# Grouped-query attention: value products in three parts, normalising on GpSimd, the first merge between turned pieces

## The reference, cut to what matters

```python
q = (hidden_states @ Wq).reshape(B, S, nh, hd).transpose(0, 2, 1, 3)
k = (hidden_states @ Wk).reshape(B, S, nkv, hd).transpose(0, 2, 1, 3)
v = (hidden_states @ Wv).reshape(B, S, nkv, hd).transpose(0, 2, 1, 3)
...
q = _apply_rope(q, cos, sin)
k = _apply_rope(k, cos, sin)
...
logits = jnp.einsum('bhqd,bhkd->bhqk', q, k) * scale
...
logits = jnp.where(causal[None, None], logits, neg)
attn = jax.nn.softmax(logits.astype(jnp.float32), axis=-1).astype(q.dtype)
out = jnp.einsum('bhqk,bhkd->bhqd', attn, v)
...
return out @ Wo
```

## Time and profile before

| | before |
|---|---|
| median of 3 runs | 2662.03 us (2660.21 to 2664.17) |
| the profiled execution | 2660.67 us |
| its span in the trace | 2658.9 us |
| busy: TensorE, VectorE, ScalarE, GpSimd | 96%, 59%, 42%, 17% |
| grouped-query stage in the trace | from about 1768 to 2593 us |

### The profile page before, as it was taken

How to read it: one execution, slowest core, us unless ns; L and a number is a source line. 1 busy time by engine, 2 the same in 40 slices (tenths; PEclk the granted TensorE clock), 3 DMA queues, 4 the chain that set the end, 5 groups by cost and what they waited for, 6 DMA issues and landing times. The chain is left out here.

```text
span 2658.9 us, 38579 instructions
## 1 busy us (share of the span) xinstructions
PE 2546.1 (96%) x12487; PEld 1843.6 (69%) x12487; DVE 1573.6 (59%) x2919; ACT 1128.3 (42%) x1832; POOL 440.4 (17%) x519
## 2 busy tenths in 40 slices
PE   6999999999999999999998779989999999999996
PEld 3666666666666666666665456667878878778774
DVE  5666666666666666666664631057557557566566
ACT  3455555555555555555554310024324324334231
POOL 0101010101010010101010000014334334343310
PEclk8899999999999999999999789989999999999998
DMA  5122121222222221212221320010010010010001
GB/s 192 42 48 53 42 50 42 53 43 50 47 45 50 44 56 42 50 42 51 45 51 51 108 73 0 0 72 24 24 39 16 24 39 16 24 39 5 12 0 52
DMA packets 46693, 116.86 MB, mean 44 GB/s; under 512 B 5313, under 2 KB 22721, under 8 KB 40514
## 3 DMA queue, kind: packets, MB, share of 16 engines
q1 hardware_dynamic: 46658, 116.40, 16.6%
HBM read 71.81 MB, written 10.49 MB: 31 GB/s over the span
## 5 line engine op out<-in xcount | busy, mean ns | idle before, releaser
L407 DVE TENSOR_REDUCE row_max<-ps_max 128x1 f32<-128x512 f32 x1024 | 672.3, 688 | 234.1 <-PE ps_max L472 204.4
L361 ACT ACTIVATE probs<-ps_score 128x1024 f32<-128x1024 f32 x512 | 525.6, 1027 | 123.6 <-PE ps_score L487 94.2
L485 PE MATMUL ps_score<-Q,K 128*128 128x512 f32 x1024 | 409.0, 399 | 0.5 <-ACT probs L361 0.5
L487 PE MATMUL ps_score<-Q,K 97*128 97x512 f32 x1024 | 405.6, 396 | 0.0
L472 PE MATMUL ps_max<-KX,Q 68*128 68x512 f32 x1024 | 379.9, 412 | 4.5 <-DVE row_max L407 2.5
L401 DVE TENSOR_TENSOR Q<-ps_x,Q 64x512 fp32r<-64x512 f32 x256 | 176.5, 690 | 240.3 <-ACT Q L356 238.5
L356 ACT ACTIVATE Q<-ps_x 64x512 fp32r<-64x512 f32 x256 | 152.0, 594 | 379.6 <-PE ps_x L457 378.2
L472 PEld LDWEIGHTS ps_max<-KX,Q 68*128 68x128 f32 x1024 | 189.1, 189 | 110.2 <-issue 53.0
L497 PE MATMUL ps_o<-probs,V_slot 128*32 128x512 f32 x2048 | 233.0, 595 | 1.1 <-ACT probs L361 1.1
L485 PEld LDWEIGHTS ps_score<-Q,K 128*128 128x128 f32 x1024 | 194.2, 190 | 55.2 <-ACT probs L361 13.3
L487 PEld LDWEIGHTS ps_score<-Q,K 97*128 97x128 f32 x1024 | 194.8, 190 | 40.9
(11 more groups left out here) (217 smaller groups left out, 3906.6 us busy)
## 6 DMA issues: line engine op xcount, KB each, us to landing
Q<-Q SPq DMA_DIRECT2D x64, 512.0 KB, 4.3
w_raw<-in_w_qrope SPq DMA_DIRECT2D x32, 512.0 KB, 3.7
wq_raw<-in_wq SPq DMA_DIRECT2D x8, 1024.0 KB, 5.6
wo_raw<-in_wo SPq DMA_DIRECT2D x8, 1024.0 KB, 4.9
w_raw<-in_w SPq DMA_DIRECT2D x6, 704.0 KB, 4.1
Q<-content_q SPq DMA_DIRECT2D x64, 64.0 KB
K<-content_k SPq DMA_DIRECT2D x64, 64.0 KB
wkv_raw<-in_wkv SPq DMA_DIRECT2D x8, 512.0 KB, 3.6
```

What stands on the lines that cost most here:

```text
L361: act.activation(probs[:, j, 2 * half:2 * half + 2, :], ps_score[half][:, :, :], ACT.Exp, scale=SCALE).then_inc(exped, 1)
L407: dve.tensor_reduce(row_max[:, t, j:j + 1], ps_max[t % 2][:, :], axis=AXX, op=ALU.max)\
L485: pe.matmul(ps_score[half][:, k, :], K1[:, b, t * P:(t + 1) * P], Q1[:, b, j, :], start=True, stop=False)
L487: last = pe.matmul(ps_score[half][:, k, :], K2[0:MROW + 1, b, j, t * P:(t + 1) * P], Q2[0:MROW + 1, b, j, :], start=False, stop=True)
```

## The change

Four things are changed, all in `gqa_stage`.

1. The values and the turned probabilities are kept in high and low parts. ScalarE's copies now write the high parts; VectorE subtracts them from PSUM to make the low ones (`low_values`, two per head, and `low_turned`, three per unit). `outputs` makes twelve fp32r matmuls per unit in place of four fp32 ones. The third turned piece and the matmuls with low probabilities wait for the low parts (`t_low`).
2. The multiplication of the probabilities with the reciprocals moves from VectorE (`normalise`) to GpSimd, with four instructions of the same widths. VectorE keeps the reciprocals (`invert`).
3. In GpSimd's list `normalise` of unit u − 2 stands behind `rope_query` of unit u; that of units 6 and 7 stands behind the loop over units.
4. The third turned piece of unit 7 stands between merge 0 and merge 1, on VectorE between the two additions to `X`.

```diff
-        V = buf("v1", [P, NB, ST, P])
+        V = [buf(f"v_{k}", [P, NB, ST, P], F32R) for k in ("hi", "lo")]
...
-        probsT = buf("probsT", [P, 3, S])
+        TURNED = [(0, S), (S, S), (2 * S, 2 * P)]
+        probsT = [buf(f"probsT_{k}", [P, 2 * S + 2 * P], F32R) for k in ("hi", "lo")]
...
+            def normalise(i, u):
+
+                pool.wait_ge(inverted, i + 1)
+                pool.sem_inc(gate_pool, 1)
+                for t in range(ST):
+                    n = (t + 1) * P
+                    ins = pool.tensor_scalar(probs[:, u % 2, t, 0:n], probs[:, u % 2, t, 0:n], inverse[:, u % 2, t:t + 1],
+                                             None, ALU.mult)
+                ins.then_inc(normed, 1)
...
                 for u in range(2, NU):
                     pool.wait_ge(scored, NU * kv + u - 1)
                     rope_query(r + u - 2, u, u % 2)
+                    normalise(NU * kv + u - 2, u - 2)
...
-                if not last:
-                    for b in range(NB):
+                for b in range(NB):
+                    normalise(NU * kv + NU - 2 + b, NU - 2 + b)
+                    if not last:
                         pool.wait_ge(scored, NU * kv + NU - 1 + b)
                         rope_key(r + NU - 2 + 2 * b, b)
                         rope_query(r + NU - 1 + 2 * b, b, 1)
...
-            def normalise(i, u):
+            def invert(i, u):
                 dve.wait_ge(exped, ONE + ST * (i + 1))
-                dve.reciprocal(inverse[:, :], sums[:, u % 2, :]).then_inc(inverted, 1)
-                dve.wait_ge(inverted, i + 1)
-                for t in range(ST):
-                    n = (t + 1) * P
-                    ins = dve.tensor_scalar(probs[:, u % 2, t, 0:n], probs[:, u % 2, t, 0:n], inverse[:, t:t + 1],
-                                            None, ALU.mult)
-                ins.then_inc(normed, 1)
+                dve.reciprocal(inverse[:, u % 2, :], sums[:, u % 2, :]).then_inc(inverted, 1)
...
+            def low_turned(i, u, k):
+                dve.wait_ge(t_high, 3 * i + k + 1)
+                at, n = TURNED[k]
+                dve.tensor_tensor(probsT[1][:, at:at + n], ps_t[(u + k) % 2][:, 0:n], probsT[0][:, at:at + n],
+                                  ALU.subtract).then_inc(t_low, 1)
...
                 maxima(i)
-                normalise(i, 0)
+                invert(i, 0)
+                for b in range(NB):
+                    low_values(kv, b)
                 rope(r, ring + ring_query(2), (START + ring_query(2)) % 2, 0, tk, 0)
                 for u in range(1, NU):
                     maxima(i + u)
-                    normalise(i + u, u)
+                    low_turned(i + u - 1, u - 1, 0)
+                    low_turned(i + u - 1, u - 1, 1)
+                    invert(i + u, u)
+                    low_turned(i + u - 1, u - 1, 2)
...
+                for k in range(2):
+                    low_turned(i + NU - 1, NU - 1, k)
                 add_out(0)
+                low_turned(i + NU - 1, NU - 1, 2)
                 add_out(1)
...
-                    pe.wait_ge(t_taken, 3 * i + 1)
+                    pe.wait_ge(t_low, 3 * i + 1)
...
-                for k, piece in enumerate(pieces):
-                    pe.wait_ge(t_taken, 3 * i + k + 1)
-                    for tile, at in piece:
-                        last = pe.matmul(ps_o[:, tile * P:S], V[:, b, tile, :], probsT[:, k, at:at + S - tile * P],
-                                         start=tile == 0, stop=k == 2)
+                for p, vs in ((0, (0, 1)), (1, (0,))):
+                    for k, piece in enumerate(pieces):
+                        pe.wait_ge((t_high, t_low)[p], 3 * i + k + 1)
+                        for v in vs:
+                            for tile, at in piece:
+                                at += TURNED[k][0]
+                                last = pe.matmul(ps_o[:, tile * P:S], V[v][:, b, tile, :],
+                                                 probsT[p][:, at:at + S - tile * P],
+                                                 start=tile == p == v == 0, stop=k == 2 and p == 1)
...
-                for k in range(3):
+                for k in range(2):
                     turn(i + NU - 1, NU - 1, k)
                 pe.wait_ge(wo_split, GQ * (kv + 1))
                 pe.wait_ge(o_low, ONE + i + NU - 1)
                 merge(last, tk, 0)
+                turn(i + NU - 1, NU - 1, 2)
                 merge(last, tk, 1)
```

More of the change, by code:

```diff
@@ L1019, in gqa_stage @@
         sums = buf("sums", [P, 2, ST])
-        inverse = buf("inverse", [P, ST])
+        inverse = buf("inverse", [P, 2, ST])
         mask = buf("mask_sb", [P, 2, P], F32R)
@@ L1043, in gqa_stage @@
         v_turned = sem("v_turned")
-        v_ready = sem("v_ready")
+        v_high = sem("v_high")
+        v_low = sem("v_low")
         summed = sem("summed")
@@ L1053, in gqa_stage @@
         turned = sem("turned")
-        t_taken = sem("t_taken")
+        t_high = sem("t_high")
+        t_low = sem("t_low")
         pv_made = sem("pv_made")
@@ L1193, in values @@
                 act.wait_ge(made, START + PER * kv + b + 1)
-                act.activation(probsT[:, b, :], ps_r[(START + b) % 2][:, :], ACT.Copy).then_inc(v_taken, 1)
+                act.activation(values_T[:, b, :], ps_r[(START + b) % 2][:, :], ACT.Copy).then_inc(v_taken, 1)
             def turned_values(kv, b):
                 act.wait_ge(v_turned, NB * kv + b + 1)
-                act.activation(V[:, b, :, :], ps_t[b][:, :].rearrange("p (t n) -> p t n", t=ST), ACT.Copy)\
-                   .then_inc(v_ready, 1)
+                act.activation(V[0][:, b, :, :], ps_t[b][:, :].rearrange("p (t n) -> p t n", t=ST), ACT.Copy)\
+                   .then_inc(v_high, 1)
             def softmax(i, u):
@@ L1269, in maxima, with low_values @@
                                       negate=True).then_inc(maxed, 1)
-            def normalise(i, u):
+            def invert(i, u):
                 dve.wait_ge(exped, ONE + ST * (i + 1))
-                dve.reciprocal(inverse[:, :], sums[:, u % 2, :]).then_inc(inverted, 1)
-                dve.wait_ge(inverted, i + 1)
-                for t in range(ST):
-                    n = (t + 1) * P
-                    ins = dve.tensor_scalar(probs[:, u % 2, t, 0:n], probs[:, u % 2, t, 0:n], inverse[:, t:t + 1],
-                                            None, ALU.mult)
-                ins.then_inc(normed, 1)
+                dve.reciprocal(inverse[:, u % 2, :], sums[:, u % 2, :]).then_inc(inverted, 1)
+            def low_values(kv, b):
+                dve.wait_ge(v_high, NB * kv + b + 1)
+                dve.tensor_tensor(V[1][:, b, :, :], ps_t[b][:, :].rearrange("p (t n) -> p t n", t=ST), V[0][:, b, :, :],
+                                  ALU.subtract).then_inc(v_low, 1)
+            def low_turned(i, u, k):
+                dve.wait_ge(t_high, 3 * i + k + 1)
+                at, n = TURNED[k]
+                dve.tensor_tensor(probsT[1][:, at:at + n], ps_t[(u + k) % 2][:, 0:n], probsT[0][:, at:at + n],
+                                  ALU.subtract).then_inc(t_low, 1)
             def low_o(i, u):
@@ L1350, in turn_values @@
                 for t in range(ST):
-                    last = pe.transpose(ps_t[b][:, t * P:(t + 1) * P], probsT[:, b, t * P:(t + 1) * P], ident[:, :])
+                    last = pe.transpose(ps_t[b][:, t * P:(t + 1) * P], values_T[:, b, t * P:(t + 1) * P], ident[:, :])
                 last.then_inc(v_turned, 1)
@@ L1437, in body @@
                     if u == 1:
-                        pe.wait_ge(v_ready, NB * (kv + 1))
+                        pe.wait_ge(v_low, NB * (kv + 1))
                     turn(i + u - 1, u - 1, 0)
```

4 lines of the change are left out of this document (2 added, 2 removed).

## The result

| | before | after |
|---|---|---|
| median | 2662.57 us (2660.21 to 2664.17) | 3121.52 us (3119.76 to 3125.19) |
| ratio | | 1.1726 (95% interval 1.1706 to 1.1747) |
| profiled span | 2658.9 us | 3123.4 us |
| mean granted clock of TensorE | 0.976 | 0.908 |

The change costs 459 us. The prediction had the sign, the circle that makes the loss and some 294 of the 459 us; the time lies 52 us above its range.

The account below looks back on a forecast made before the run. TensorE was taken as the bound, made to wait by a chain through GpSimd's queue. 2660.7 us plus 201 for chains and heads' ends gave 2862, plus 94 for the clock 2956; range 2848 to 3070.

Parts of the forecast that it names:

- the sign: Whole kernel: the change makes it slower, given a chance of 0.93.
- the circle that makes the loss: Grouped-query unit: transposes, projection, narrow low part, rotation, query parts, normalising, back to transposes; 11.79 us, TensorE waiting 3.65.
- the price of normalising on GpSimd: Four multiplications per unit on GpSimd, read from a line of copy, cast and select: 1.80 us.
- The upper bound: Normalising on GpSimd at the rate of its two-input subtraction, times 2.1: 3.8 us per unit.
- two-input rate: Rival: GpSimd multiplies at its two-input rate, 2.0 us more on 48 chains, 3052 us; chance 0.20.
- the clock: TensorE's clock halves for 3.4 us after each of 55 waits, losing 1.7 us each: 94 us.
- a head's end: First merge waits for unit 6's low part behind two rotations: 2.35 us later at seven heads, 16 us.
- units 6 and 7 go free: A head's last two units have no late query ahead in GpSimd's queue, so they only save 2 × 0.2 us.
- the products' saving: Value products on TensorE in three part products: 0.2 us per unit, 13 us if TensorE stays the bound.
- the moved merge: Head's end: the merge between turned pieces fills the last piece's wait with nothing new, since the merge itself waits longer.
- if GpSimd's sum is over 2.5, its price is: Check on the new profile: if GpSimd's multiplications sum to over 2.5 us, the price taken for them is wrong.
- faster: Rival: normalising on GpSimd is hidden in its slack and the products' 13 us are left, 2648 us; chance 0.04.

Follow-up runs that it names:

- e4_number: The changed kernel with GpSimd multiplying by the constant 1.0 in place of the per-row reciprocal, normalisation left out; 3081.42 us, 1.1581.
- e3_fill: The changed kernel with 30 or 20 matmuls that nothing reads put into TensorE's wait for normalised probabilities in units 0 to 5; 3001.86 us, 1.1279.
- e5_two_inputs: The changed kernel with GpSimd's normalising written as a two-input multiplication, the reciprocal broadcast along the row; 3011.75 us, 1.132.
- e14_between_turned: e6_on_scalar with unit 0 normalised before the second values copy, unit 6's low part inside the first rotation, unit 7's first wide one before the second; 2648.26 us.
- e2_ahead: The changed kernel with GpSimd, inside a head, normalising the unit two back before making the query's high and low parts; 2717.05 us, 1.021.
- e10_before_low_first: The kernel before with only the low part of unit 6's output moved ahead of the two rotations on VectorE; 2672.06 us, 1.0038.
- e6_on_scalar: The changed kernel with normalising on ScalarE instead of GpSimd, behind the narrow turned piece and ahead of the outputs' high part; 2684.31 us, 1.0089.

## Why the prediction was wrong, and where it was right

**The step that failed first: the price of normalising on GpSimd.** 1.80 us was taken, 3.8 was the upper bound, and 4.27 is the measured stretch. The working put a copy, a cast and a select on one line and read the multiplication from it. That these three lie on a line says nothing on a fourth operation; the select that decided the choice costs 294 ns at 128x128, the multiplication 605. The upper bound took the two-input subtraction for the dearest that could come, and the scalar multiplication lies above it: 1565 ns for 512 columns against 1270. On 48 circles that is 48 × 2.47 = 119 us. The rival "two-input rate", 3052, came nearest, and its reason, that the scalar per row makes the price, is not the one that `e4_number` left standing. The page of the Trainium skill that the prediction weighed (GPSIMD Engine Reference, "Engine selection") advised rightly against the move. It has GpSimd about twice as slow for two inputs and roughly at line rate for one; the trace differs, with 4.27 us for VectorE's 1.28, 3.3 times, for an operation with one tensor input.

**The term that was mis-sized next: the clock.** 55 waits at 1.7 us made 94. Filling 48 of them gave back 120, 26 more than all 55 were to cost, and 38 more than the 82 of these 48. The slow stretch was taken as 3.4 us long, from the earlier trace rows; after these longer waits it is 6.8 us at 0.50 (10.2 in 21 of the 55) and covers the transposes and the whole projection: 2.38 us in the unit shown, between the 1.7 taken and the 3.66 that the prediction had as its worst.

**What was left out: a head's end.** With the right price and without the clock the prediction's sum gives 2862 + 119 = 2981; `e3_fill` has 3002, 21 more, and of these the clock term had 7 × 1.7 = 12 for the merges that `e3_fill` leaves slow. Inside a head it agrees (14.27 for 14.26, the first unit with a wait 16.91 − 8.24 = +8.67 for 6.26 + 2.47), so the 21 us lie at the head's end: its last stretch is 4.65 us longer in after and 3.6 to 4.8 in `e3_fill` (5.5 in the last head), against a forecast of 2.35 − 0.4 (in the last head a saving alone). The second head's end in after shows why:

```profile
2074.86 1.09 PE L1407 MATMUL ps_t<-ident,probs 128*128 128x128 f32 x8 [2.21 <-POOL probs L1155]
...
2078.17 2.07 PE L1432 MATMUL ps_r<-wo_hi,o_hi 128*128 128x512 f32 x4 [2.22 <-DVE o_lo L1305]
...
2083.45 0.43 PE L1407 MATMUL ps_t<-ident,probs 128*128 128x128 f32 x2
```

The prediction let units 6 and 7 go free. With 2.47 us less on GpSimd this wait of 2.21 would not be there (with 1.46 less, in `e5_two_inputs`, it is 0.7); at 4.27 the last unit's transposes wait too. And the first merge, after its wait, takes 5.3 us to the next transposes, all at a granted clock of 0.50, where it takes 2.85 in `e14_between_turned`. So the miss of 165 is 119 for the price, 26 for the clock and 21 for a head's end. That they add up proves nothing by itself, since 26 and 21 are what was left between the same sum and the same runs; the prices, waits and stretches above are what shows them.

**What held.** The circle and its order (`e2_ahead` opens it and takes 404 us off), and the sum of its other links, to 0.01 us in `e3_fill` (single links are off by up to 0.1 and cancel, which is luck); the products' saving, 0.2 forecast and 0.25 measured and lost where TensorE waits. What the prediction says of the moved merge was not tried in after itself; beside low parts on faster engines it is worth 36 us. The test that the prediction set itself ("if GpSimd's sum is over 2.5, its price is") is the one that came true. The rival "faster", 2648 if normalising is hidden, is what `e14_between_turned` shows at 2648.26: on another engine, and only after two waits at a head's end had been found and taken away. That the numbers agree is luck: five units of a head save 0.25 us each, its end 1.27, the prediction left the wait there as it was, and the unit with the first transposes loses 0.8.

## What to carry to other kernels

When work goes to another engine, ask first what already stands in that engine's list and whether any of it waits for the engine that is to be relieved: a list in a fixed order closes a circle, and then every microsecond of the moved work is paid once a round. A price that no row shows is not bounded by the rows of other operations, however well they lie on a line; give it a range beyond the dearest of them. A step that is waited for under two conditions (data and a buffer) gains nothing until both are early.

## What the runs showed of the hardware

- GpSimd, fp32, 128 partitions, 128 to 512 columns: scalar multiplication 2.5 ns a column and some 0.29 us besides (0.21 with a constant), the same beside a busy and an idle VectorE; multiplication with a broadcast second input 1.67 ns a column and 0.19 us; a cast of 512 columns 0.61 us, a subtraction of two tensors 1.27. The form with the fewest inputs was the dearest.
- ScalarE scales the same four pieces in 1.91 us, VectorE in 1.28.
- Idle times of TensorE of 5.9 us came with a granted clock of 0.50 for 6.8 us, at times 10.2; in the unit shown 1.8 of the 6.8 still lay in the idle time. Behind shorter waits, equally long at each head's end, the clock fell to half at some ends and not at others: 1.3 us at one of seven (before), 1.93 at four of seven (`e10_before_low_first`), behind 4.05 it fell at all seven (`e6_on_scalar`). Matmuls that nothing reads, put into the wait, kept the clock at 1.00 and made the kernel 120 us faster.
